# A graph layer with a mixture of experts on one core: rows turned by transposing DMAs instead of TensorE

## Chip, cores and metric

One NeuronCore of a Trainium2 chip runs the whole layer as one program. The metric is the device time of one execution in microseconds (us).

## What is computed

The reference, cut to the parts that the change touches (1250 tokens of 1024 features, 8 experts of which each token takes 2):

```python
xn = _layernorm(x)
x = x + gnn(xn, edges) + mix(xn, W_qkv, ..., W_out, b_out)      # graph product and linear attention
z = _layernorm(x)
t = z * rsqrt(mean(z * z) + 1e-5) * norm_scale                  # rows that gate and experts read
logits = t @ gate_w + gate_b                                    # 1024 x 8
top_v, top_i = top_k(logits, 2); probs = softmax(top_v)
for each expert e:
    h = swiglu(t @ w1[e] + b1[e])                               # 1024 -> 512 -> 256
    y = h @ w2[e] + b2[e]                                       # 256 -> 1024
    acc = acc + w[:, e] * y
out = x + z + acc
```

Float32 in and out. Large products are made of f16 halves: a value is a high part plus a low part, and three products (high-high, high-low, low-high) stand for one.

## The kernel before

Five engines run programs of their own and meet at semaphores; each engine takes its instructions strictly in the order in which they are written, so the order inside the loops below is the schedule. SyncE (SP) issues plain DMAs, GpSimd (POOL) does some sums and issues the gathers and the adding scatters. Two stages matter here.

**The mix stage**, tiles of TT = 125 tokens, i = 2 to 9 in a loop (tiles 0 and 1 are started in the stage ahead). In `mix_tile` TensorE adds 96 products of 512 columns for tile i (`graph_part`, L933, and `attend_part`, L939), with four small float32 products `attend_unit` (L890) for a later tile between them; tiles 8 and 9 have none. Beside it:

- VectorE: four times `attend_unit` (L1686 to L1688: add, reciprocal, multiply), `add_half` twice (L1723, takes TensorE's sums out of a bank; TensorE waits for it before it writes that bank again), `mix_norm(i - 1)` (L1727 to L1741), which makes the rows t of the tile before in `tm` and raises `t_ready`, and `gate` (L1745).
- In the same tile 4 to 6 *quarters* of expert weights are split for later use, 40 in all: SP asks for a float32 quarter (`quarter_ask`, L535, two buffers), ScalarE writes its high half (L1322), VectorE its low half (L1749), and SP stores both (`next_quarters`, L541) and asks for the next but one.
- ScalarE: `attend_hi` (L1272), two small roots, and `tt_copy` (L1316). POOL: `attend_lo` (L639), `mix_out` (L655, on which the store of the base rows waits) and `mix_in` (L651, adds the bias to the x rows of the next tile).
- The gate: `gate_tile` (L987) turns tile i - 1 of t by eight float32 transposes on TensorE into PSUM, ScalarE copies them to `tt`, and `gate_logits` (L994) makes the logits by eight float32 products of 8 columns. SP stores t and the base rows (`store_mixed`, L395), and t is read back by the experts.

Then the routing works out which token goes where.

**The expert stage**: 27 blocks of 128 rows. For block b: POOL gathers 128 rows of t (`gather`, L696) into one of two buffers `rows`; TensorE turns them by eight float32 transposes (`row_T`, L1024) into PSUM; ScalarE copies the f16 high half (`row_hi`, L1359), VectorE the low half (`row_lo`, L1880) to `rowT`; TensorE multiplies, 24 products in two halves (`up`, L1033); VectorE and ScalarE apply swiglu; TensorE turns the result (`act_T`, L1041) between the halves of the next block's `up`, ScalarE and VectorE split it (L1364, L1899), and `down` is 12 products (L1051). VectorE evacuates (L1907), ScalarE scales by the gate's weight (`scale_y`, L1373), and POOL adds the rows to the output by an accumulating scatter (`add_block`, L706). Each scatter waits for the one before to have landed (`y_added`). TensorE's order in a block is `row_T(b + 1)`, first half of `up(b)`, `act_T(b - 1)`, second half of `up(b)`, `down(b - 1)`. POOL's is: wait for the buffer, `gather(b + 2)`, `add_block(b - 2)`. Weights of an expert are loaded by SP while the experts before run.

## Time and profile before

| | us |
|---|---|
| median of 3 runs | 1025.75 |
| the runs | 1019.88 to 1029.12 |
| profiled execution, its own time | 1022.55 |
| its span, first to last instruction | 1020.8 |
| mix stage, tiles 2 to 9 (from t of tile 1 to t of tile 9) | 511 to 716 |
| expert stage (from the first turned row to the end) | 752 to 1021 |

The profile lists for each engine when it was busy and what ended its waits. A busy TensorE is not one at its peak; a wait is put down to whatever signal came last. The chain of waits is followed back from the last instruction, so it names what set the end, while busy shares are means over stages.

### The profile page before, as it was taken

How to read it: one execution, taken by the hardware profiler on the slowest of the kernel's cores; microseconds unless marked ns; L12 is line 12 of the kernel's file. 1: busy time of each engine (PE TensorE's matmuls, PEld its weight loads, DVE VectorE, ACT ScalarE, POOL GpSimd, SP SyncE). 2: the span in 40 equal slices, each digit the busy share in tenths (PEclk: the TensorE clock that was granted, in tenths of full speed). 3: DMA queues.
4: the chain of work that ended last, by engine and by line, in shares of the span. 5: the costliest groups of instructions: out<-in, count | busy, mean ns of one | idle time of the engine just before them, and what ended most of it. 6: DMA issues, size and time to landing. Idle time of an engine off the chain costs nothing.

```text
span 1020.8 us, 16203 instructions
## 1 busy us (share of the span) xinstructions
PE 922.0 (90%) x5361; PEld 576.2 (56%) x5362; DVE 708.9 (69%) x1198; ACT 366.5 (36%) x621; POOL 173.5 (17%) x210
## 2 busy tenths in 40 slices
PE   3998999999999999998998999998359999999992
PEld 2555667766665654555665666665335455555551
DVE  4867999999999974378856777755455455555551
ACT  5657666666441114431122222222112233333331
POOL 1000000000000000015222223322122233323322
PEclk9999999999999999999999999999569999999997
DMA  9735676666663009910255555566459978886544
GB/s 303 227 92 167 201 221 213 194 195 191 213 199 123 22 22 231 336 53 1 61 163 148 159 161 158 151 175 172 177 197 311 315 185 251 270 252 144 123 83 62
DMA packets 89162, 176.59 MB, mean 173 GB/s; under 512 B 24824, under 2 KB 39160, under 8 KB 89088
## 3 DMA queue, kind: packets, MB, share of 16 engines
q1 hardware_dynamic: 81328, 147.50, 46.1%
q0 software_dynamic: 7776, 28.32, 12.4%
q8 instruction: 37, 0.61, 0.3%
q14 instruction: 21, 0.17, 0.1%
HBM read 113.63 MB, written 62.67 MB: 173 GB/s over the span
## 4 chain that ended last, share of the span: by engine, by line
PE 41%; DVE 20%; DMA 18%; ACT 6%; issue 5%; POOL 4%; SPq 3%; DVEq 1%; POOLq 0%; ACTq 0%
PE bank L758 10%; PE windows L1033 9%; DMA arena<-in_w_flat 7%; PE bank L907 7%; DMA arena<-t_dram,arena 6%; PE bank L1051 4%; DVE arena L1687 2%; POOL arena L655 2%; DMA out_x<-arena 2%; DVE arena L1510 2%; PE bank L1024 2%; SPq L541 2%; DMA arena<-in_w_qkv 2%; PE windows L790 2%; DVE arena L1520 2%
## 5 line engine op out<-in xcount | busy, mean ns | idle before, releaser
L758 PE MATMUL bank<-arena 128*125 128x512 f16 x960 | 217.0, 384 | 10.2 <-DVE arena L1483 10.2
L758 PEld LDWEIGHTS bank<-arena 128*125 128x125 f16 x960 | 130.5, 138 | 84.2 <-issue 11.3
L1033 PE MATMUL windows<-arena 128*128 x648 | 149.5, 381 | 0.0
L907 PE MATMUL bank<-arena 128*128 128x416 f16 (+1 forms) x576 | 105.7, 338 | 2.0 <-DMA arena<-split_dram 2.0
L1033 PEld LDWEIGHTS windows<-arena 128*128 128x128 f16 x648 | 63.7, 98 | 65.6 <-issue 1.4
L933 PE MATMUL bank<-arena 128*125 128x512 f16 x432 | 96.3, 379 | 3.8 <-DVE arena L1723 2.3
L939 PE MATMUL bank<-arena 128*125 128x512 f16 x432 | 97.5, 384 | 0.0
L1749 DVE SCALAR_TENSOR_TENSOR arena<-arena 128x512 f16<-128x512 f32 x40 | 39.3, 982 | 61.8 <-ACT arena L1322 61.8
L907 PEld LDWEIGHTS bank<-arena 128*128 128x128 f16 x576 | 55.0, 97 | 45.5 <-DMA arena<-split_dram 2.4
L933 PEld LDWEIGHTS bank<-arena 128*125 128x125 f16 x432 | 58.7, 137 | 37.8 <-DVE arena L1723 2.7
L939 PEld LDWEIGHTS bank<-arena 128*125 128x125 f16 x432 | 59.7, 138 | 34.3 <-issue 1.6
L1051 PE MATMUL bank<-arena 128*128 x324 | 74.3, 379 | 2.2 <-DVE arena L1899 2.2
L639 POOL TENSOR_TENSOR arena<-arena 128x250 f16<-128x250 f32 x40 | 26.6, 665 | 261.1 <-ACT arena L1272 261.1
L1687 DVE RECIPROCAL arena<-arena 128x250 f32<-128x250 f32 x40 | 68.7, 1717 | 1.4
L706 POOL DMA_INDIRECT out_x<-arena x27 | 43.3, 1605 | 150.6 <-ACT arena L1373 88.2
L1272 ACT ACTIVATE arena<-arena 128x250 f16<-128x250 f32 x40 | 16.5, 412 | 140.7 <-DVE arena L1688 140.7
L1510 DVE TENSOR_TENSOR arena<-windows,arena 128x1024 f32 x49 | 59.7, 1219 | 6.8 <-PE windows L791 3.9
L1359 ACT ACTIVATE arena<-bank 128x512 f16<-128x512 f32 x54 | 29.3, 594 | 78.7 <-PE bank L1024 71.0
L790 PE MATMUL windows<-arena 128*128 128x128 f16 x392 | 50.6, 219 | 5.4 <-ACT windows L1188 5.2
L1887 DVE SCALAR_TENSOR_TENSOR arena<-windows,arena 128x512 f32<-128x512 f32 x27 | 18.7, 691 | 51.7 <-PE windows L1033 51.7
L1051 PEld LDWEIGHTS bank<-arena 128*128 128x128 f16 x324 | 31.7, 98 | 40.4 <-issue 2.5
L1520 DVE SCALAR_TENSOR_TENSOR arena<-arena 128x1024 f16<-128x1024 f32 x44 | 53.5, 1216 | 1.1 <-ACT arena L1133 1.1
(248 smaller groups left out, 1428.1 us busy)
## 6 DMA issues: line engine op xcount, KB each, us to landing
arena<-split_dram SPq DMA_DIRECT2D x56, 512.0 KB, 5.5
arena<-in_w_flat SPq DMA_DIRECT2D x44, 512.0 KB, 4.5
split_dram<-arena SPq DMA_DIRECT2D x88, 256.0 KB, 4.6
arena<-in_w_flat SPq DMA_DIRECT2D x40, 256.0 KB, 4.5
split_dram<-arena SPq DMA_DIRECT2D x80, 128.0 KB, 2.3
arena<-in_x SPq DMA_DIRECT2D x20, 448.0 KB
arena<-in_w_qkv SPq DMA_DIRECT2D x8, 1024.0 KB, 11.7
t_dram<-arena SPq DMA_DIRECT2D x10, 448.0 KB
```

Source lines behind the costliest of these rows:

```text
L706: pool.indirect_dma_start(out=out, out_offset=bass.IndirectOffsetOnAxis(ap=to_idx[s], axis=0), in_=ysb[s], in_offset=None, compute_op=ALU. ...
L758: mm = pe.matmul(bank[b][0:TT, :], xt[:, l, k, tok(i)], wkv[:, r, k, c0:c0 + 512], start=(k == 0 and n == 0), stop=(k == KT - 1 and n == 2))
L790: pe.matmul(o, key_hi, lo, start=False, stop=False, skip_group_check=True)
L907: mm = pe.matmul(bank[u % 3][:, 0:n], wq[h][:, l, k, :], xt[:, r, k, a:a + n], start=(k == 0 and c == 0), stop=(k == KT - 1 and c == 2))
L933: pe.matmul(o[half][0:TT, :], xt[:, l, k, tok(i)], wg[:, r, k, c0:c0 + 512], start=(k == 0 and c == 0), stop=False)
L939: mm = pe.matmul(o[half][0:TT, :], ut16[:, k, bass.ds(2 * t + l, 1), h * TT:(h + 1) * TT].rearrange("p o n -> p (o n)"), wo[:, r, k, c0:c0 ...
L1033: mm = pe.matmul(bank[6][:, :], rowT[s][:, l, k, :], arena16[:, bass.ds(off + (r * KT + k) * 512, 512)], start=(k == 0 and c == 0), stop=( ...
L1051: mm = pe.matmul(bank[half][:, :], actT[:, l, k, :], arena16[:, bass.ds(off + 8192 + r * 2048 + k * D + half * 512, 512)], start=(k == 0 a ...
L1510: v.tensor_tensor(w_acc[:, bass.ds(at[0], G * P)], windows[:, :], w_acc[:, bass.ds(at[0], G * P)], ALU.add).then_inc(acc_done, 1)
L1520: v.scalar_tensor_tensor(part[h][:, 1, :], stage[h], SW, part[h][:, 0, :], ALU.mult, ALU.subtract).then_inc(piece_done, 1)
L1687: st.done(v.reciprocal(a, a))
L1749: v.scalar_tensor_tensor(quarter_part[q % 2][:, 1, :], quarter[q % 2], SW, quarter_part[q % 2][:, 0, :], ALU.mult, ALU.subtract).then_inc( ...
```

## The change

Both turns leave TensorE and become DMAs of a crossbar, issued by ScalarE's queue, which write the turned f16 data to SBUF directly.

- Mix stage: t is split into f16 halves before it is turned: `split_hi` on ScalarE (one copy of 1024 columns) and `split_lo` on VectorE (one subtraction of 1024) write `t_hl`, which SP stores in place of the float32 rows (the same bytes). `gate_turn` turns [128, 2048] f16 in one DMA. The logits are sixteen f16 products: eight of 16 columns, the high half with both halves of the gate's weights, and eight of 8 columns. `gate` is two instructions. `gate_tile` and `tt_copy` are gone.
- In SP's `next_quarters` the ask for the next but one quarter stands ahead of the two stores.
- POOL zeroes `t_hl` once, ahead of the sum of the biases, since 3 of its 128 partitions hold no token.
- VectorE's and ScalarE's orders in a mix tile are new (rows below). TensorE does `gate_logits(0)` ahead of tile 2, and `gate_logits(i - 1)` behind tile i.
- Expert stage: `turn` turns the gathered [128, 2048] f16 rows in one DMA to `rowT`. `row_T`, `row_hi` and `row_lo` are gone. POOL waits for the turn in place of TensorE before it gathers into a buffer again, and `up` waits for the turn.

```diff
-            def gate_tile(i, h):
-                pe.wait_ge(t_ready, i + 1)
...
-                    mm = pe.transpose(bank[4 + k // 4][:, (k % 4) * TT:(k % 4 + 1) * TT], tm[h][0:TT, k * P:(k + 1) * P], ident[0:TT, 0:TT])
...
             def gate_logits(i):
-                pe.wait_ge(tt_done, 2 * (i + 1))
+                pe.wait_ge(tt_in, 16 * (i + 1))
                 pe.wait_ge(gate_done, START + i)
                 for k in range(KT):
-                    mm = pe.matmul(bank[6][0:TT, 0:E], tt[:, k, :], gate_f[:, k * E:(k + 1) * E], start=(k == 0), stop=(k == KT - 1))
+                    pe.matmul(bank[6][0:TT, 0:2 * E], tt[:, k, 0:TT], gate16[:, k, :], start=(k == 0), stop=False)
+                for k in range(KT):
+                    mm = pe.matmul(bank[6][0:TT, 0:E], tt[:, KT + k, 0:TT], gate16[:, k, 0:E], start=False, stop=(k == KT - 1))
                 mm.then_inc(gate_mm, 1)
-            gate_tile(0, 0)
-            pe.wait_ge(mixc_in, 80)
+            pe.wait_ge(gate_lo, 1)
+            gate_logits(0)
             for i in range(2, NT):
                 mix_tile(i, i % 2, i // 2, attend=i < NT - 2)
-                gate_logits(i - 2)
-                gate_tile(i - 1, 1 - i % 2)
...
+                gate_logits(i - 1)
             gate_logits(NT - 1)
...
+            def gate_turn(i):
+                a_.wait_ge(t_lo, i + 1)
                 a_.wait_ge(gate_mm, START + i)
...
+                a_.dma_start_transpose(tt, t_hl[i % 2].rearrange("p a b -> p (a b)")).then_inc(tt_in, 16)
...
                 for q in qs:
                     sp.wait_ge(quarter_lo, q + 1)
+                    if q + 2 < QUARTERS:
+                        quarter_ask(q + 2)
                     for hl in range(2):
                         sp.dma_start(quarter_rows(split_dram[hl], q), quarter_part[q % 2][:, hl, :]).then_inc(quarter_out[q % 2], 16)
-                    if q + 2 < QUARTERS:
-                        quarter_ask(q + 2)
...
+            pool.wait_ge(m_mm, 2 * KT)
+            for h in range(2):
+                pool.memset(t_hl[h], 0.0).then_inc(t_clear, 1)
...
-                    pool.wait_ge(rt_psum, 2 * t + h + 1)
+                    pool.wait_ge(turn_in[h], 16 * (t + 1))
                     gather(2 * t + h + 2, h)
                     add_block(2 * t + h - 2, h)
...
-            def row_hi(b, s, first=False):
-                a_.wait_ge(rt_psum, b + 1)
+            def turn(b, s, q, first=False):
+
+                a_.wait_ge(row_in[s], 16 * (q + 1))
                 if not first:
                     a_.wait_ge(h_mm, b - 1)
...
+                a_.dma_start_transpose(rowT[s], rows[s]).then_inc(turn_in[s], 16)
...
-                    row_hi(b + 1, 1 - h)
+                    turn(b + 1, 1 - h, t + 1 + h)
                     act_hi(b - 1)
                     scale_y(b - 2, h)
                     sigmoid(b)
```

VectorE, a mix tile with `attend_unit` (L1686 to L1688), from `gate` (L1745) on; L1749 is a quarter's low half, L1723 `add_half`. Before:

```order
L1745 SCALAR_TENSOR_TENSOR arena<-windows,arena 125x8
L1749 SCALAR_TENSOR_TENSOR arena<-arena 128x512
L1686 TENSOR_TENSOR arena<-bank,arena 128x250
L1687 RECIPROCAL arena<-arena 128x250
L1688 SCALAR_TENSOR_TENSOR arena<-arena 128x250
L1749 SCALAR_TENSOR_TENSOR arena<-arena 128x512
L1686 TENSOR_TENSOR arena<-bank,arena 128x250
L1687 RECIPROCAL arena<-arena 128x250
L1688 SCALAR_TENSOR_TENSOR arena<-arena 128x250
L1749 SCALAR_TENSOR_TENSOR arena<-arena 128x512
L1723 SCALAR_TENSOR_TENSOR arena<-bank,arena 125x512
```

The same stretch of the changed kernel, behind its `gate`; there L1690 to L1692 are `attend_unit`, L1749 is `split_lo`, L1758 a quarter's low half, L1727 `add_half`:

```order
L1690 TENSOR_TENSOR arena<-bank,arena 128x250
L1691 RECIPROCAL arena<-arena 128x250
L1692 SCALAR_TENSOR_TENSOR arena<-arena 128x250
L1749 TENSOR_TENSOR arena<-arena 125x1024
L1690 TENSOR_TENSOR arena<-bank,arena 128x250
L1691 RECIPROCAL arena<-arena 128x250
L1692 SCALAR_TENSOR_TENSOR arena<-arena 128x250
L1758 SCALAR_TENSOR_TENSOR arena<-arena 128x512 x2
L1690 TENSOR_TENSOR arena<-bank,arena 128x250
L1691 RECIPROCAL arena<-arena 128x250
L1692 SCALAR_TENSOR_TENSOR arena<-arena 128x250
L1758 SCALAR_TENSOR_TENSOR arena<-arena 128x512 x2
```

The first quarter now stands behind two attend units and `split_lo`, the quarters come in pairs, four of them stand ahead of the first `add_half` where three did, and the attend unit that stood ahead of `mix_norm` stands behind it.

ScalarE, one block of the expert loop (L1359 `row_hi`, L1364 `act_hi`, L1373 `scale_y`, L1369 the sigmoid). Before:

```order
L1359 ACTIVATE arena<-bank 128x512 x2
L1363 REGISTER_ALU
L1364 ACTIVATE arena<-windows 128x256
L1373 ISA
L1373 ACTIVATE arena<-arena 128x1024
L1367 REGISTER_ALU
L1369 ACTIVATE arena<-arena 128x256
```

And of the changed kernel (L1368 `act_hi`, L1377 `scale_y`, L1373 the sigmoid):

```order
L1363 DMA_TRANSPOSE arena<-arena 128x16x128
L1367 REGISTER_ALU
L1368 ACTIVATE arena<-windows 128x256
L1377 ISA
L1377 ACTIVATE arena<-arena 128x1024
L1371 REGISTER_ALU
L1373 ACTIVATE arena<-arena 128x256
```

The issue of the turn stands where the two copies stood, ahead of `act_hi`.

## Rows read from the trace of the kernel before

**Rows 1.** The page: busy time of each engine.
```profile
PE 922.0 (90%) x5361; PEld 576.2 (56%) x5362; DVE 708.9 (69%) x1198; ACT 366.5 (36%) x621; POOL 173.5 (17%) x210
```
**Rows 2.** By stretch: length, busy PE, PEld, DVE, ACT, POOL (instructions), PE clock, DMA share, GB/s.
```profile
595.70:622.60 26.90, 25.50 (x130) 17.14 (x128) 19.97 (x28) 6.00 (x13) 8.21 (x6) 1.00 0.57 155
848.00:857.00 9.00, 9.00 (x48) 4.76 (x47) 5.57 (x12) 3.14 (x6) 3.11 (x4) 1.00 0.98 311
962.00:971.00 9.00, 9.00 (x48) 4.76 (x47) 5.18 (x11) 2.92 (x5) 3.34 (x5) 1.00 0.53 117
```
**Rows 3.** Timeline, a mix tile: start, length, engine, line, count [idle before, releaser].
```profile
595.71 1.29 DVE L1741 SCALAR_TENSOR_TENSOR arena<-arena 125x1024 f32<-125x1024 f32 x1
...
597.08 2.81 POOL L655 TENSOR_TENSOR arena<-arena 125x1024 f32<-125x1024 f32 x1 [3.43 <-DVE arena L1741]
...
599.91 0.77 SPq L395 DMA_DIRECT2D out_x<-arena  x2
...
601.20 0.73 DVE L1749 SCALAR_TENSOR_TENSOR arena<-arena 128x512 f16<-128x512 f32 x1 [1.00 <-ACT arena L1322]
...
602.21 0.43 SPq L535 DMA_DIRECT2D arena<-in_w_flat  x1
...
603.10 0.78 SPq L395 DMA_DIRECT2D arena<-in_x  x2
...
607.84 0.63 ACT L1322 ACTIVATE arena<-arena 128x512 f16<-128x512 f32 x1 [2.93 <-DMA arena<-in_w_flat]
608.50 0.69 DVE L1749 SCALAR_TENSOR_TENSOR arena<-arena 128x512 f16<-128x512 f32 x1 [4.04 <-ACT arena L1322]
...
609.85 0.69 PE L890 MATMUL bank<-arena 128*128 128x250 f32 x2 [1.17 <-DVE arena L1723]
...
614.58 2.24 DVE L1749 SCALAR_TENSOR_TENSOR arena<-arena 128x512 f16<-128x512 f32 x1
...
622.60 1.29 DVE L1741 SCALAR_TENSOR_TENSOR arena<-arena 125x1024 f32<-125x1024 f32 x1
```
**Rows 4.** The chain of waits: start, length, what.
```profile
144.72 1.37 PE bank L765 x24
...
469.19 2.32 POOL arena L646
...
714.73 1.28 DVE arena L1741
...
722.66 3.54 PE windows L994 x16
...
873.96 9.55 DMA arena<-t_dram,arena
...
892.63 0.87 PE bank L1024 x8
893.51 2.59 PE windows L1033 x12
...
995.95 6.08 DMA out_x<-arena
```
**Rows 5.** Timeline of POOL in the expert stage: two scatters.
```profile
882.02 1.60 POOL L706 DMA_INDIRECT out_x<-arena  x1 [6.86 <-DMA out_x<-arena]
...
889.99 1.61 POOL L706 DMA_INDIRECT out_x<-arena  x1 [4.15 <-ACT arena L1373]
```
**Rows 6.** Groups by line: count | busy, mean ns of one | idle before.
```profile
L1669 DVE TENSOR_TENSOR arena<-arena 128x1024 f16<-128x1024 f32 x8 | 9.4, 1221 | 1.3 <-ACT arena L1262 1.3
...
L628 POOL MEMSET arena<- 128x1024 f32 x1 | 1.0, 952 | 295.3 <-PE bank L758 295.3
```
**Rows 7.** DMA issues over the span: count, KB each, median us to landing.
```profile
arena<-split_dram SPq DMA_DIRECT2D x56, 512.0 KB, 5.5
...
wg_dram<-arena SPq DMA_DIRECT2D x16, 256.0 KB, 3.8
...
arena<-in_kn_w SPq DMA_DIRECT2D x1, 512.0 KB, 14.0
```

More of the change, by code:

```diff
@@ L1341, in _ @@
+                quarter_split(qs[0])
+                gate_turn(i - 1)
+                quarter_split(qs[1])
+                if attend:
+                    attend_hi(4 * h + 2, t + 1, unit + 2)
+                for q in qs[2:4]:
                     quarter_split(q)
[L1342 to L1345 removed]
+                if attend:
+                    attend_hi(4 * h + 3, t + 1, unit + 3)
```

165 lines of the change are left out of this document (73 added, 92 removed).

## The prediction

> **What bounds the kernel now.** I read the page first. TensorE is busy for 90% of the span [rows 1], which invites the reading that whatever leaves TensorE leaves the time. The stretches and the chain say where that holds.
>
> In the mix stage it does not quite. A tile takes 26.9 us and TensorE is busy for 25.50 of them [rows 2] (from one finished t to the next, 595.71 to 622.60 [rows 3]), but it waits 1.17 us in each tile for VectorE's `add_half` [rows 3]. `add_half` was late because it is queued behind a quarter: VectorE idled 4.04 us for ScalarE, which had idled for the quarter's DMA, asked for at 602.21 and landed 5.6 us later, at 607.8 [rows 3]. So one tile of VectorE is 19.97 us of work [rows 2], 6.0 of waits for quarters (4.04, and twice the 1.00 that a quarter waits right behind an attend unit, because ScalarE must first do `attend_hi` and then the quarter's high half [rows 3]) and 0.9 of small gaps: 26.9. VectorE with the quarters' round trip is the loop that closes last; TensorE has hardly more than a microsecond in hand.
>
> In the expert stage TensorE does set the pace. The chain runs over `row_T` (0.87), and three groups of twelve products at 2.59 [rows 4], with 0.2 for `act_T` a block of 8.86 us. But a second loop is close: each scatter waits for the one before. Alone it lands in 6.08 us [rows 4], and with 0.9 for POOL's wake-up, index and issue that is 7.0 from one to the next. At 882.02 a scatter had waited 6.86 us for the one before it; the next, 7.97 us later, waited for ScalarE, so the one in flight had then landed in under 7.2 [rows 5]. And a gather of 9.55 us ended on the chain [rows 4], so gathers are no earlier than needed. DMA is 0.98 busy where weights load and 0.53 in late blocks [rows 2].
>
> **The change, part by part.**
>
> *TensorE in a mix tile.* Eight float32 logits go, 1.77 us at full clock (half of the 3.54 that they took at half clock [rows 4]), and eight turns, 0.87 like those of a block [rows 4]. Sixteen f16 products come; 24 narrow f16 ones took 1.37 us, 57 ns each [rows 4], so 0.9. TensorE's work falls from 25.5 to 23.8 us. That is worth nothing in time while VectorE's tile is longer.
>
> *VectorE in a mix tile.* It gains `split_lo`, 1.22 us by its like [rows 6], and 0.2 for the second gate instruction: 21.4. The row of 2.24 us [rows 3] is a quarter stretched by POOL's sum beside it, which now falls behind the quarters: 1.55 less, so 19.8, with the gaps 20.7. The waits in the new order, counted from a finished t: gate 0.3, attend unit 2.5 (between the end of the first quarter, about 597.7, and 600.2, where the wait of 1.00 begins [rows 3]), `split_lo` 1.2, attend unit 2.5, wait 1.0 for ScalarE, quarter 0.7: the first quarter ends at 8.2. The second waits 0.45 (the turn's issue stands between, taken like SP's 0.43 [rows 3]) and ends at 9.3, the attend unit behind it at 11.9. The third quarter was asked for at 8.3, now ahead of its stores. I take 4.2 us to land, between 3.8 [rows 7] and the 5.6 above; with ScalarE's 0.63 it is there at 13.1: wait 1.2. The fourth is held up in SP's queue. Ahead of its ask stand the x rows, which wait until the base rows have landed, and these wait for POOL's sum of 2.81 [rows 3], now queued behind an `attend_lo` whose attend unit comes after t: the sum ends at 6.9, the store lands 3.2 after its issue (599.91 to 603.10 [rows 3]) at 10.1, the x rows' issue takes 0.8, and 5.6 later, at 16.5, the fourth quarter lands. With 0.7 for ScalarE it is ready at 17.2, VectorE at 14.0: wait 3.2. The fifth stands right behind an attend unit: 1.0. Waits 6.9, tile 20.7 + 6.9 = 27.6: 0.7 more than 26.9, in six tiles +4. Lower bound: the fourth quarter lands with the third, tile 24.4, six tiles -15; TensorE's 23.8 would stop it there. Upper: the last quarter still meets POOL's sum, +1.55 a tile, +13. In tiles 8 and 9, without attend units, the earlier ask and `split_lo` about cancel.
>
> *Ahead of tile 2.* `gate_logits(0)` now waits for a first turn. TensorE can spare this, but VectorE stands at `gate(0)` and the next attend unit: two halves of t at 1.22 each, 0.45, 5.5 to land and 0.9 of products are 9.3 us from its last work on tile 1, of which it fills 7 with `mix_norm`, `split_lo` and the gate's weights: +2. With a turn that lands in 14.0 [rows 7] it would be +10.
> POOL's zeroing is two fills of 4 KB a partition, 0.95 each [rows 6], ahead of a sum that is on the chain [rows 4]: +2, +4 if f16 costs by the element, 0 if an attend unit hides it.
>
> *Behind tile 9.* Before, from t (714.73 + 1.28) to the end of the last logits (722.66 + 3.54) 10.2 us [rows 4]. Now 1.2 + 1.2 + 0.45 + 5.5, and 1.8 of products at half clock, 10.2: nothing. With 3.8 to land -1.7, with 14.0 +8.5.
>
> *Expert stage.* TensorE's block is 8.86 - 0.87 = 8.0. ScalarE's and VectorE's two copies go, which nothing waited for. A turn needs three prices, none of which the trace shows. To land: 5.5, like the other 512 KB [rows 7], between 3.8 and 14.0. Of the DMA engines: at 311 GB/s with a share of 0.98 [rows 2] 512 KB are 1.7 us. Of ScalarE's queue: 0.45, at most twice the 1.6 of a scatter's issue [rows 5], 3.2. Late blocks have room: 0.53 x 9 = 4.8 us of DMA work and 1.7 are 6.5 in 8.0, and the scatter, 7.0 from one to the next, becomes at most 8.7. The turn is used a block after its gather lands, so 9.55 + 0.5 + 5.5 = 15.5 us fit into the two blocks (16.0) that a gather has; the buffer is free again just as late. In about 17 blocks I give TensorE its 0.87: -15. In the other ten or so weights load, the DMA engines are full [rows 2], and 512 KB more must be paid: some +1 each, since the loads themselves have slack, +10. The first block waits for a gather and a turn in place of a gather and copies: +2. Sum -3. Both ends: 27 x 0.87 = -23; and all 27 blocks at a scatter of 8.7 + 1.7 are +40.
>
> *A rule of the skill here.* The Trainium skill, "DMA: Bandwidth & Descriptors", section "Latency and other measured facts", gives 261 GB/s for a transposing DMA with a non-contiguous middle dimension. By that 512 KB are an estimated 2.0 us of the engines against my 1.7, so +3 in the ten loaded blocks. No run here shows it yet.
>
> **Sum.** Against the profiled execution, 1022.55 us: +4 +2 +2 +0 -3 = +5, 1027.6. That execution lies 3.2 below the median of the runs (1025.75); I put the new time at 1028, which is no change as far as a measurement of this kernel can tell (about 1%).
>
> **Rivals.**
>
> *A, faster.* The quarters land early enough and TensorE becomes the bound in both stages. For it: the ask stands ahead of the stores, an earlier `add_half` is what the 1.17 us of TensorE ask for [rows 3], and late blocks have DMA to spare [rows 2]. Against it: SP's queue behind the x rows, as worked out, and a scatter loop that is already at 7 to 8 us. Time: six tiles at 24.4 or so, -15 (in place of +4), the expert stage -15, the fixed +4 and 0 of the tail: -26, near 997; with half of either gain near 1010.
>
> *B, slower by the issue.* ScalarE is held for 3.2 us by each turn's issue. In a mix tile that stands between two quarters (+1.5 a tile after what the fourth quarter's wait absorbs, +12); in a block it stands ahead of `act_hi`, which is due 2.8 us after the block starts (one 2.59 and `act_T`). The gather lands about when the block starts, so the issue ends 0.4 late, up to 1 where gathers are late: 27 x 0.8 = +21. Time 1028 + 33 = 1061. It decides from an issue of about 2.5 us on. For it: a turn has more pieces than any plain DMA here. Against: a plain issue of 128 rows takes 0.43.
>
> *C, slower by the crossbar.* A turn takes 14 us or more. Then gather, turn and release of a buffer are a loop, (9.55 + 0.5 + 14 + 1.5) / 2 = 12.8 us a block, 27 x 3.9 = +105, with +8 and +8 at the two ends of the mix stage: near 1145. It decides from about 6 us on, above which each microsecond costs half of one a block. For and against it no row speaks but the 14.0.
> The Trainium skill, "VectorE: DVE Perf Modes", section "The three transpose paths", has 1309 ns for one 128x128 f16-sized block through the crossbar and 390 ns on TensorE. If sixteen went one behind another, the estimate would be 20.9 us a turn, which is this case and worse; if that figure is mostly fixed cost, it is my case. No run here tells yet.
>
> **How the numbers follow.** Chances: my forecast 0.35 (its own range 1014 to 1042), A 0.33, B 0.21, C 0.11. Of the forecast's share 0.22 lies within 1%, 0.10 above and 0.03 below; of A 0.02 within. Faster 0.34, within 1% 0.24, slower 0.42. The range leaves out C and the best end of A: 1000 to 1075.
>
> **What would show it.** In the mix stage: intervals between finished t of 27 to 28 us against 26.9, TensorE's work near 24 in each with some 4 idle before L890 or the graph products, and VectorE's longest wait ahead of the fourth quarter. If the interval is 25 or less, my reading of SP's queue is wrong. In the expert stage: blocks of 8.0 us late and 9 to 11 where weights load; scatters that wait for the one before more often than seven times in 27; the issue row of the turn under 0.6 us on ScalarE, its landing near 5.5. An issue above 2.5 is B, blocks of 11 us or more also late, with TensorE waiting for the turn, is C. POOL's two fills and the first turn should show as 4 us ahead of t of tile 1 and tile 2.

## The result: 11% slower, and the profile after

| | before | after |
|---|---|---|
| median, us | 1027.37 | 1147.6 |
| the runs | 1019.88 to 1029.12 | 1134.43 to 1173.72 |
| ratio | | 1.114 [1.105, 1.122] |
| profiled execution, its own time | 1022.55 | 1173.72 |

I had forecast 1028 with a range of 1000 to 1075. That is wrong: the time lies 120 us above the forecast and 73 above the range. The profiled execution after is the longest of its four, by 25 us and more; the other three alone enter the ratio. Its rows show mechanisms; how much each part costs is taken from the timed runs below.

The page after: busy time, the span in 40 slices (TensorE's clock and the DMA engines), and the queue that carries the turns. The same row of before is in [rows 1].

```profile
PE 929.4 (79%) x5065; PEld 550.9 (47%) x5066; DVE 689.8 (59%) x1165; ACT 338.6 (29%) x558; POOL 174.9 (15%) x212
...
PEclk9999999999999999879899998855888966888997
DMA  9454677666510891026666666646999999998984
...
DMA packets 166122, 195.98 MB, mean 167 GB/s; under 512 B 101785, under 2 KB 116121, under 8 KB 166049
...
q10 hardware_dynamic: 76960, 19.40, 13.4%
```

TensorE is as busy as before, 929 us against 922, although it does 296 instructions fewer: its granted clock falls in both stages. The 37 turns are 76,960 packets, 2080 each. Their packets took 13.4% of 1172 us, which is 157 us of all sixteen engines or 4.2 us a turn, where I had 1.7. (This "engine time" is the time that packets took by the profile. It is no fixed price, as the runs below show.) In the expert stage the DMA row stands at 9 nearly throughout.

The groups of the page that lost most, busy and mean ns of one, then the idle time before them and what ended it:

```profile
L1023 PE MATMUL windows<-arena 128*128 x648 | 165.1, 410 | 85.9 <-DMA arena<-arena 84.3
...
L1041 PE MATMUL bank<-arena 128*128 x324 | 85.2, 419 | 22.2 <-DVE arena L1898 22.2
...
L1758 DVE SCALAR_TENSOR_TENSOR arena<-arena 128x512 f16<-128x512 f32 x40 | 32.1, 802 | 77.4 <-ACT arena L1315 77.4
```

L1023 is `up`. TensorE waits 84 us for turns (`arena<-arena`) and 22 us for the split of act, which waits for ScalarE. In the mix stage VectorE waits for quarters.

One mix tile after, to be laid beside [rows 3] (timeline: start, length, engine, line, count [idle before, releaser]); t of two tiles stands first and last, L1303 is the turn's issue, L1315 and L1758 the halves of a quarter, L1727 `add_half`:

```profile
557.12 1.28 DVE L1745 SCALAR_TENSOR_TENSOR arena<-arena 125x1024 f32<-125x1024 f32 x1
...
565.67 4.20 ACTq L1303 DMA_TRANSPOSE arena<-arena  x1
...
569.97 0.63 ACT L1315 ACTIVATE arena<-arena 128x512 f16<-128x512 f32 x1 [3.55 <-issue]
...
570.63 0.69 DVE L1758 SCALAR_TENSOR_TENSOR arena<-arena 128x512 f16<-128x512 f32 x1 [3.45 <-ACT arena L1315]
...
578.73 0.63 ACT L1315 ACTIVATE arena<-arena 128x512 f16<-128x512 f32 x1 [3.92 <-DMA split_dram<-arena]
...
579.39 0.69 DVE L1758 SCALAR_TENSOR_TENSOR arena<-arena 128x512 f16<-128x512 f32 x1 [3.81 <-ACT arena L1315]
580.00 0.68 DVE L1727 SCALAR_TENSOR_TENSOR arena<-bank,arena 125x512 f32<-125x512 f32 x1
...
580.74 1.20 PE L896 MATMUL bank<-arena 128*128 128x250 f32 x2 [5.34 <-DVE arena L1727]
...
581.74 7.72 PE L939 MATMUL bank<-arena 128*125 128x512 f16 x24
...
588.92 1.28 DVE L1745 SCALAR_TENSOR_TENSOR arena<-arena 125x1024 f32<-125x1024 f32 x1
```

The tile takes 31.8 us (26.9 before). The issue takes 4.20 us of ScalarE, so VectorE waits 3.45 us for the second quarter. It waits 3.81 us for the fourth, because ScalarE waits for the *store* of the quarter two before it. `add_half` stands behind both, and TensorE waits 5.34 us. Its granted clock is then low, 0.64 from 580.7 to 588.7 us: 24 products take 7.72 us, where 24 like them take 5.34 us at a clock of 1.00.

### The profile page after: what moved, and what is told of

Its sections match the earlier page's. It is cut to its first block, busy times and chain, and to the rows that moved or that the text cites. A ratio compares the mean times of both kernels' runs of the same rounds, so it can differ in the third digit from the quotient of the medians.

```text
span 1172.0 us, 15535 instructions
## 1 busy us (share of the span) xinstructions
PE 929.4 (79%) x5065; PEld 550.9 (47%) x5066; DVE 689.8 (59%) x1165; ACT 338.6 (29%) x558; POOL 174.9 (15%) x212
## 3 DMA queue, kind: packets, MB, share of 16 engines
q10 hardware_dynamic: 76960, 19.40, 13.4%
q0 software_dynamic: 7776, 28.32, 12.1%
## 4 chain that ended last, share of the span: by engine, by line
PE 31%; DMA 28%; DVE 20%; issue 7%; ACT 6%; ACTq 3%; POOL 2%; SPq 2%; DVEq 1%; POOLq 0%
DMA arena<-arena 12%; PE bank L764 9%; DMA arena<-t_dram,arena 7%; PE bank L913 6%; DMA split_dram<-arena 5%; PE windows L1023 4%; DVE arena L1691 3%; ACTq L1363 3%; PE bank L939 3%; PE bank L945 2%; DMA arena<-in_w_qkv 2%; DVE arena L1514 2%; DVE arena L1524 1%; DMA out_x<-arena 1%; PE bank L1041 1%
## 5 line engine op out<-in xcount | busy, mean ns | idle before, releaser
L1023 PE MATMUL windows<-arena 128*128 x648 | 165.1, 410 | 85.9 <-DMA arena<-arena 84.3
L764 PE MATMUL bank<-arena 128*125 128x512 f16 x960 | 217.4, 384 | 11.1 <-DVE arena L1487 11.1
L764 PEld LDWEIGHTS bank<-arena 128*125 128x125 f16 x960 | 130.6, 138 | 85.4 <-issue 12.3
L1023 PEld LDWEIGHTS windows<-arena 128*128 128x128 f16 x648 | 67.5, 104 | 171.4 <-issue 113.9
L939 PE MATMUL bank<-arena 128*125 128x512 f16 x432 | 113.1, 426 | 12.8 <-DVE arena L1727 11.3
L1898 DVE TENSOR_TENSOR arena<-windows,arena 128x256 f16<-128x256 f32 x27 | 11.4, 424 | 167.1 <-ACT arena L1368 167.1
L1041 PE MATMUL bank<-arena 128*128 x324 | 85.2, 419 | 22.2 <-DVE arena L1898 22.2
L945 PE MATMUL bank<-arena 128*125 128x512 f16 x432 | 98.4, 386 | 0.0
L939 PEld LDWEIGHTS bank<-arena 128*125 128x125 f16 x432 | 66.8, 155 | 56.5 <-issue 18.6
L913 PEld LDWEIGHTS bank<-arena 128*128 128x128 f16 x576 | 55.8, 98 | 47.3 <-issue 3.0
L1758 DVE SCALAR_TENSOR_TENSOR arena<-arena 128x512 f16<-128x512 f32 x40 | 32.1, 802 | 77.4 <-ACT arena L1315 77.4
L1368 ACT ACTIVATE arena<-windows 128x256 f16<-128x256 f32 x27 | 10.3, 383 | 232.5 <-PE windows L1031 133.8
L945 PEld LDWEIGHTS bank<-arena 128*125 128x125 f16 x432 | 60.2, 139 | 35.0 <-issue 2.5
L642 POOL TENSOR_TENSOR arena<-arena 128x250 f16<-128x250 f32 x40 | 29.2, 730 | 307.1 <-ACT arena L1259 307.1
L1041 PEld LDWEIGHTS bank<-arena 128*128 128x128 f16 x324 | 34.0, 105 | 68.8 <-issue 38.3
## 6 DMA issues: line engine op xcount, KB each, us to landing
arena<-in_w_qkv SPq DMA_DIRECT2D x8, 1024.0 KB, 11.3
```

Of the source, the lines that this page charges most:

```text
L764: mm = pe.matmul(bank[b][0:TT, :], xt[:, l, k, tok(i)], wkv[:, r, k, c0:c0 + 512], start=(k == 0 and n == 0), stop=(k == KT - 1 and n == 2))
L913: mm = pe.matmul(bank[u % 3][:, 0:n], wq[h][:, l, k, :], xt[:, r, k, a:a + n], start=(k == 0 and c == 0), stop=(k == KT - 1 and c == 2))
L939: pe.matmul(o[half][0:TT, :], xt[:, l, k, tok(i)], wg[:, r, k, c0:c0 + 512], start=(k == 0 and c == 0), stop=False)
L945: mm = pe.matmul(o[half][0:TT, :], ut16[:, k, bass.ds(2 * t + l, 1), h * TT:(h + 1) * TT].rearrange("p o n -> p (o n)"), wo[:, r, k, c0:c0 ...
L1023: mm = pe.matmul(bank[6][:, :], rowT[s][:, l * KT + k, :], arena16[:, bass.ds(off + (r * KT + k) * 512, 512)], start=(k == 0 and c == 0), ...
L1041: mm = pe.matmul(bank[half][:, :], actT[:, l, k, :], arena16[:, bass.ds(off + 8192 + r * 2048 + k * D + half * 512, 512)], start=(k == 0 a ...
```

## Experiments: where the 120 us are

First the split between the stages, then the mix stage, then the experts. Edits are against the changed kernel unless said otherwise; lines left out of a cut are marked "...". A ratio is to the kernel before, run beside the experiment; its median was 1024 to 1026 us each time. The theories: S, the issue of a turn holds ScalarE; O, the new order of VectorE makes TensorE wait; D, a turn takes too much of the DMA engines, which are full; Q, of these, above all in the queue of an expert's weights; L, gather and turn one behind the other are too long for two buffers.

**Old experts (`e1_old_experts`).** The new mix stage, the experts of before.

```diff
+                for k in range(KT):
+                    mm = pe.transpose(bank[2 + 2 * s + k // 4][:, (k % 4) * P:(k % 4 + 1) * P], rows[s][:, k * P:(k + 1) * P], ident)
...
-                a_.dma_start_transpose(rowT[s], rows[s]).then_inc(turn_in[s], 16)
```

> The new mix stage with the experts of before (eight float32 turns on TensorE, float32 rows of t stored), so that the loss is split between the two stages. In the profile of the changed kernel t of tile 9 comes 47.8 us later than before, and the last logits another 5 us: all theories put this run near 1025 + 53 = 1078 us (1065 to 1085), and the experts' share then is the other 65 us. If it is under 1050 most of the loss in the mix stage belongs to something else than the change (a disturbed profile), if over 1100 the experts lost little.

Measured 1070.1, ratio 1.046 [1.040, 1.052]. The mix stage costs 44 us, the experts the other 76 (I had read 65 from the profiles).

**Turned by TensorE in the mix stage too (`e3_tensor_turn`).** e1 with the float32 turn and logits of before.

```diff
+                    mm = pe.transpose(bank[4 + k // 4][:, (k % 4) * TT:(k % 4 + 1) * TT], tm[h][0:TT, k * P:(k + 1) * P], ident[0:TT, 0:TT])
...
-                a_.dma_start_transpose(tt, t_hl[i % 2].rearrange("p a b -> p (a b)")).then_inc(tt_in, 16)
```

> As e1, but t is turned on TensorE and the logits are the float32 products of before; the new order on VectorE and ScalarE, the ask ahead of the stores, both halves of t (still computed, read by nobody) and the zeroing stay. Theory S (the turn's issue, about 4 us, holds ScalarE between two quarters and in front of the first root): the turn is gone, so only the zeroing (3.6 us) and the halves of t (up to 1.2 us a tile) are left: 1030 to 1040. Theory O (the new order of VectorE puts its waits in front of TensorE, whoever turns): the tiles stay at 30 us and more, 1060 or above.

1049.3, 1.024 [1.019, 1.029]: between the two. The turn, with the f16 logits that hang on it, is 21 us of the 44, and 23 remain without any turning DMA, more than S and less than O had said.

**Before, with the ask ahead of the stores (`e5_before_ask_ahead`).**

```diff
                     sp.wait_ge(quarter_lo, q + 1)
+                    if q + 2 < QUARTERS:
+                        quarter_ask(q + 2)
                     for hl in range(2):
                         sp.dma_start(quarter_rows(split_dram[hl], q), quarter_part[q % 2][:, hl, :]).then_inc(quarter_out[q % 2], 16)
-                    if q + 2 < QUARTERS:
-                        quarter_ask(q + 2)
```

> The kernel before with one edit: SP asks for the next but one quarter ahead of the two stores. In e3 ScalarE waited 27 us in five tiles for the stores of a quarter to land (before: for the quarter's own DMA, 38 us). If the ask ahead of the stores is part of the 24 us that e3 loses: slower than before by 5 to 15 us, 1031 to 1041. If the new order of VectorE is all of it: 1022 to 1030.

A miss in sign: 1012.6, ratio 0.988 [0.983, 0.992]. This one edit of the change is a gain of 13 us and beats both kernels. Between 540 and 700 us TensorE is now busy for 159.6 of the 160 us (150.6 before), so it is the bound there.

**The new order alone (`e14_order_alone`).** e5 and the new order of VectorE and ScalarE.

```diff
-                quarter_split(qs[2])
...
+                for q in qs[2:4]:
+                    quarter_split(q)
                 add_half(i, h, 0)
-                attend_unit(4 * h + 3, t + 1, unit + 3)
-                quarter_split(qs[3])
-                add_half(i, h, 1)
+                if attend:
+                    attend_unit(4 * h + 3, t + 1, unit + 3)
```

> The kernel before with the ask ahead of the stores (e5, 1012.6 us) and the new order of VectorE and ScalarE in a mix tile, without the halves of t and without the zeroing: all that stands between e5 and e3 (1049.3) but these two. Theory O (the pair of quarters ahead of the first add_half makes TensorE wait): most of the 36.7 us are here, 1035 to 1045. If the halves of t (VectorE 1.2 us, ScalarE 1.0 a tile) and the zeroing (3.6 us) are most of it: under 1028.

1039.4, 1.015 [1.011, 1.018]: the order costs 27 us, the halves of t and the zeroing the other 10. Waits from 540 to 700 us in e5, then in e14 (who waited, for whom, us in total, times, longest; L1749 and L1769 are a quarter's low half, L1322 and L1332 its high half, L1739 is `add_half`):

```profile
ACT arena L1322 <- DMA split_dram<-arena: 39.0, 16, 8.4
DVE arena L1749 <- ACT arena L1322: 38.1, 22, 6.3
...
PE bank L890 <- DVE arena L1688: 0.2, 1, 0.2
```
```profile
DVE arena L1769 <- ACT arena L1332: 45.3, 21, 7.0
ACT arena L1332 <- DMA split_dram<-arena: 33.5, 11, 10.4
...
PE bank L894 <- DVE arena L1739: 8.2, 4, 2.2
```

In e5 TensorE waits for next to nothing. In e14 it waits 8.2 us for `add_half`, which stands behind two quarters in a row, and 2.1 us for attend units, and its granted clock is 0.95 in this stretch against 1.00. ScalarE waits for stores in both, no longer in e14 (33.5 us) than in e5 (39.0), so it is not these waits by themselves that cost, but where they stand. There are two quarter buffers, and each is free only when its store has landed. With an attend unit between two quarters (the old order) VectorE has work in that time; with two pairs ahead of `add_half` the wait falls in front of it. That the pairing does it is argued from these rows; I did not move it by itself.

**SP issues the turn in the mix stage (`e2_sp_turn`).** e1 with the issue moved off ScalarE.

```diff
             def store_mixed(i):
                 h = i % 2
+                sp.wait_ge(t_lo, i + 1)
+                sp.wait_ge(gate_mm, START + i)
+                apart(sp)
+                sp.dma_start_transpose(tt, t_hl[h].rearrange("p a b -> p (a b)")).then_inc(tt_in, 16)
```

> e1 with the turn of the mix stage issued by SP (ahead of the store of t) in place of ScalarE, and earlier by up to 5 us. Theory S: ScalarE no longer stands 4 us between two quarters; SP's queue stands instead, ahead of the stores and asks, where some of it comes back: faster than e1 by 5 to 15 us, 1055 to 1065. Theory D (the turn's packets delay the quarter's own transfers): within 4 us of e1, 1066 to 1074. If SP's queue is the scarcer one (my reading of the fourth quarter): slower, over 1075.

1063.9, 6 us less than e1. The place on ScalarE is at most a third or so of the turn's 21, since more has moved than the place: SP issues the turn earlier, and it then takes 1.6 us to issue and 3.7 to land at the median, against 4.0 and 8.2 in the changed kernel. What the 15 us are that stay with so short a turn, the runs do not show.

**The f16 logits without the turning DMA (`e18_narrow_logits`).** e5, TensorE turns, ScalarE and VectorE split the turned rows.

```diff
+                    ins = v.tensor_tensor(tt[:, 1, 4 * b:4 * b + 4, :], bank[4 + b][:, 0:4 * TT].rearrange("p (k n) -> p k n", n=TT),
+                                          tt[:, 0, 4 * b:4 * b + 4, :], ALU.subtract)
```

> A version meant to be faster than both kernels: e5 (before with the ask ahead, 1012.6 us; TensorE there hardly waits any more in a mix tile) with the sixteen f16 products of the change but the turns on TensorE: ScalarE copies the high half of the turned rows out of PSUM, VectorE subtracts the low half (some 1.3 us a tile, where it has 38 us of waits in six tiles). TensorE's tile is 0.9 us shorter: eight tiles, less 1.5 behind the last one: 1005 to 1010. If VectorE with the quarters closes last again: 1012 to 1020.

1019.3, 0.994 [0.992, 0.996]: better than before, not than e5. The tiles with attend units take 26.2 us (25.3 to 26.2 in e5). TensorE waits 9.3 us for VectorE's attend units between 540 and 700 us, where e5 had 0.2: the 0.9 us a tile that TensorE saves are worth nothing while VectorE gains work.

**The ladder (`e13_ladder`).** The price of a turn alone, in the routing stage of before.

```diff
+            for cols in (2048, 0, 1024, 512, 128, 2048):
+                if cols:
+                    a_.dma_start_transpose(bias_b.bitcast(F16)[:, 0:cols].rearrange("p (k n) -> p k n", n=P), scale_b.bitcast(F16)[:, 0:cols]).then_inc(spare_turn, 16)
+                else:
+                    a_.dma_start(bias_b, scale_b).then_inc(spare_turn, 16)
```

> The kernel before, with six transfers one behind another (each waited for) on ScalarE's queue during the routing, when the other queues are nearly quiet: turns of 2048 columns, a plain copy of 512 KB, turns of 1024, 512, 128 and again 2048 columns. If the 4 us of the issue and 8 us to land in the mix stage are the price of a turn's own packets: issue 4, 2, 1, 0.4 us and landing 8, 5, 3.5, 2.5, in proportion to the columns plus some 2 us. If they come from other transfers beside it: here the issue of 2048 columns is under 2 us and lands in 4 (the shortest of the mix stage landed in 3.9 with an issue of 1.6). The time of the kernel stays at 1026 or rises by up to 10, where the ladder reaches into the first gathers.

The issues on ScalarE's queue (start, length), then for the stretches of the first three the packets, MB and share of the sixteen engines, and the time to land:

```profile
729.86 1.44 ACTq L1359 DMA_TRANSPOSE arena<-arena  x1
734.25 0.53 ACTq L1361 DMA_DIRECT2D arena<-arena  x1
737.23 1.26 ACTq L1359 DMA_TRANSPOSE arena<-arena  x1
```
```profile
q10 hardware_dynamic: 2080, 0.52, 62.8%
...
arena<-arena ACTq DMA_TRANSPOSE x1, 4.4
...
q10 hardware_dynamic: 144, 0.52, 42.6%
...
arena<-arena ACTq DMA_DIRECT2D x1, 512.0 KB, 3.0
...
q10 hardware_dynamic: 1056, 0.26, 43.9%
...
arena<-arena ACTq DMA_TRANSPOSE x1, 3.1
```

Alone, a turn holds ScalarE for 1.44 us, lands in 4.4 and takes 0.628 x 4.4 = 2.8 us of the engines (the second of 2048 columns, last in the ladder: 2.02 us and 4.3); the plain copy takes 0.426 x 3.0 = 1.3. The kernel's time stayed at 1026.5. The second guess was right: the 4 us and 8 us of the mix stage come from what is under way beside it. A turn alone is cheap against those, though more than twice the plain copy, and its 2.8 us of the engines are already above my 1.7.

**Smaller weight loads (`e7_after_small_loads`).** It leaves out nearly all weights of experts 3 to 7 and computes with what the buffers hold.

```diff
-                        sp.dma_start(to, split_dram[hl, m + n]).then_inc(s, 16)
+                        if e < 3:
+                            sp.dma_start(to, split_dram[hl, m + n]).then_inc(s, 16)
+                        else:
+                            sp.dma_start(to[:, 0:16], split_dram[hl, m + n, :, 0:16]).then_inc(s, 16)
```

> The changed kernel with nearly all of the weights of experts 3 to 7 left out (16 of 2048 columns are loaded, the buffers keep older weights), so the engines carry no loads in most of the expert stage. Leaves out work. Theory Q: blocks of 8.0 to 8.5 us from expert 2 on, no wait of TensorE for a turn over 3 us, issues of 1.5 to 3 us: 1075 to 1095 in all. Theory S: an issue of 4 us in front of the copy of act to f16 stays in each block, so blocks stay at 9.5 or more: 1115 or above.

1127.1 in a single run: only some 20 us less, and TensorE still waited 61.7 us for turns, in 17 waits of up to 12.1. Q's burst of weight packets is not the main cause. The stretch from 880 to 1080 us, with hardly a weight under way, and its queues of gathers and scatters (q0) and of turns (q10), columns as in [rows 2] and as in the page above:

```profile
880.00:1080.00 200.00, 167.56 (x728) 74.87 (x726) 71.24 (x152) 34.88 (x57) 58.02 (x77) 0.93 1.00 166
...
q0 software_dynamic: 5510, 20.08, 52.4%
q10 hardware_dynamic: 38820, 9.78, 41.0%
```

The DMA share is 1.00 all the same. These are 19 blocks and 38,820 / 2080 = 18.7 turns, so gather and scatter take 0.524 x 200 / 19 = 5.5 us of the engines a block and a turn 0.41 x 200 / 18.7 = 4.4, together 9.9 us, where TensorE needs 8.0. This fits theory D without Q.

**Paced loads (`e6_paced_loads`).**

```diff
                         sp.dma_start(to, split_dram[hl, m + n]).then_inc(s, 16)
+                        if e > 0:
+                            sp.wait_ge(s, 128 * e + 16 * (3 * hl + n + 1))
```

> The changed kernel, in which the loads of an expert's weights (from expert 1 on) wait for each other: one piece of 512 KB is under way at a time instead of six and two biases. Theory Q (the turn's 2080 packets of 256 bytes stand in the DMA engines' queues behind the packets of the loads, so it lands after 14 to 24 us while six pieces are under way): the waits of 15 to 18 us of TensorE go, some 40 us less, near 1100, and the longest wait of TensorE for a turn is under 8 us. Theory S (what costs is the 4 us on ScalarE's queue): no change, 1135 to 1150. If the pieces one by one no longer keep up with the experts, TensorE waits for a weight instead, and the time rises.

1213.5, 1.189 [1.181, 1.197], slower still. The waits for turns fell from 84 to 54 us, the longest to 11.3 (Q had under 8), but TensorE then waited 78 us for weights: pieces one at a time do not keep up.

**A turn nobody needs (`e9_extra_turn`), and the same issued later (`e15_extra_behind`).** e1 and one more turn, of zeros, in 24 blocks; e15 has it behind `scale_y`.

```diff
                     row_hi(b + 1, 1 - h)
+                    a_.wait_ge(spare_turn, 16 * (b - 1))
+                    extra_turn()
                     act_hi(b - 1)
                     scale_y(b - 2, h)
```

> e1 (experts as before, TensorE turns) with one more turning DMA of [128, 2048] f16 in each of 24 blocks, of zeros, into memory that nobody reads: only ScalarE waits, for the one a block earlier. Theory D (the sixteen DMA engines are full: by the profile a turn takes 4.6 us of all of them, gather and scatter 5, loads 3 a block, together more than a block of 8.9): near e1 + 24 x (11.5 - 8.9) = 1070 + 62 = 1132 us (1115 to 1145), although nothing needs the turn. Theory L (gather, turn and release of the buffer are a loop, and its length is what costs): e1 + 0 to 10, at most 1080. Theory S (ScalarE is held by the issue ahead of its copy of act): e1 + 24 x 1 = about 1095.

> e9 (1197 us) with the extra turn issued behind ScalarE's copy of act and its scaling of y, not ahead of them. In e9 TensorE waited 49 us for the split of act (ScalarE was in the issue for up to 12 us) and 57 us for gathers that landed late. Theory S (the time on ScalarE's queue): the 49 us and what hangs on them go, 1130 to 1150. Theory D (the turn's packets slow every other transfer; ScalarE's waits only follow): 1180 or more.

e9 1196.9, 1.160 [1.148, 1.171]; e15 1124.0, 1.095 [1.084, 1.105]. The extra turn costs 127 us ahead of `act_hi`, more than any theory had, and 54 behind, less than S or D had said for that: a price on ScalarE and one beside it are both there. The flaw of both: ScalarE also waits for the extra turn of one block earlier, 43 us in e9 and 27 in e15.

**Plain copies in its place (`e12_extra_plain`, `e16_extra_pieces`).** Both against e9.

```diff
-                a_.dma_start_transpose(bias_b.bitcast(F16).rearrange("p (k n) -> p k n", n=P), scale_b.bitcast(F16)).then_inc(spare_turn, 16)
+                a_.dma_start(bias_b, scale_b).then_inc(spare_turn, 16)
```
```diff
-                a_.dma_start_transpose(bias_b.bitcast(F16).rearrange("p (k n) -> p k n", n=P), scale_b.bitcast(F16)).then_inc(spare_turn, 16)
+                a_.dma_start(view(198656, [2 * KT, P], F16), view(203552, [2 * KT, 2 * P], F16)[:, :, 0:P]).then_inc(spare_turn, 16)
```

> e9 with the extra turn replaced by a plain copy of the same 512 KB from the same memory to the same memory, issued at the same place by ScalarE's queue. What is in dispute: whether a turn is dear for its bytes or for its 2080 packets of 256 bytes. By bytes (my own price, 1.7 us of the sixteen engines): it would cost about as much as the turn, e9's 1197 less little, 1180 or more. By packets: the copy has few large ones, costs 1.7 us of the engines a block where they are full, so e1 + 10 to 25: 1080 to 1095.

> e12 (plain copy, 1079 us) with the same 512 KB copied in pieces of 256 bytes, 2048 of them, from pieces that lie 512 bytes apart, still without turning. If the price of a turn is that of small packets: near e9, 1170 or more. If it is that of the turning itself (2 bytes at a time through the crossbar, or what the queue does for it): near e12, 1075 to 1100.

The plain copy 1079.2 (+9), the one in pieces 1115.9 (+46), with 59 us of ScalarE's waits for it, the same flaw.

**The flaw mended (`e19_free_turn`, `e20_free_pieces`).** Three places to write to, and a wait for the transfer of three blocks earlier; the cut is e19 against e9. e20 has the plain copy in pieces in the turn's place.

```diff
-                    a_.wait_ge(spare_turn, 16 * (b - 1))
-                    extra_turn()
+                    a_.wait_ge(spare_turn[u % 3], 32 * t + 16 * (u // 3 + 1))
+                    extra_turn(u % 3)
```

> e9 (1197 us) with its flaw mended: there ScalarE waited, ahead of its copy of act, for the extra turn of one block earlier, which late landings made 43 us. Now there are three places to write to, and it waits for the turn of three blocks earlier. What is left is the turn's issue on ScalarE and its share of the DMA engines. If both stay as dear as in e9: 1197 - 43 = 1154 or more. If most of e9 was that wait and what followed from it: 1100 to 1130, near e15 (1124).

> e16 (1116 us, plain pieces of 256 bytes) mended in the same way; its wait for the extra copy was 59 us on ScalarE. If small packets as such slow the other transfers: 1090 or more. If they cost nothing but their own late landing: near e12 (1079), 1072 to 1085; the difference to e19 is then the turning itself, its issue and its engine time.

The turn 1185.7, 1.156 [1.149, 1.164], +116 to e1; the pieces 1080.9, 1.058 [1.052, 1.064], +11. So neither bytes nor small packets are dear here: the same 512 KB in 256-byte pieces cost about what a plain copy costs, 0.5 us a block, the turning 4.8. Stretches of the expert stage of e1, of e20 and of e19 (columns as in [rows 2]; the last three are TensorE's clock, DMA share, GB/s):

```profile
830.00:1030.00 200.00, 195.87 (x1013) 102.42 (x1012) 110.60 (x220) 64.13 (x111) 68.80 (x89) 1.00 0.78 214
```
```profile
830.00:1040.00 210.00, 199.12 (x1014) 103.33 (x1012) 110.25 (x221) 64.27 (x110) 68.58 (x88) 0.98 1.00 264
```
```profile
830.00:1130.00 300.00, 209.48 (x949) 105.02 (x948) 104.47 (x207) 59.88 (x103) 64.22 (x84) 0.84 0.96 173
```

With the pieces the engines are full and move 264 GB/s; with the turns they are as full and move 173. Length times share is the engine time of a stretch: 156 us in e1, 210 in e20, 288 in e19. What e20 adds just fits beside TensorE's work, what e19 adds does not. The queue of the turns and extra transfers on the pages of e1 (which has the ten turns of the mix stage only), e20 and e19:

```profile
q10 hardware_dynamic: 20800, 5.24, 3.4%
```
```profile
q10 hardware_dynamic: 70336, 17.83, 9.0%
```
```profile
q10 hardware_dynamic: 70720, 17.83, 12.4%
```

Less e1's 36 us, a copy in pieces took (97 - 36) / 24 = 2.5 us of the engines and a turn (148 - 36) / 24 = 4.6 (in e15, by the same sum, 3.2). The other transfers slow down too, but less: the packets of the two large queues, the same in all three, took 602 us of the engines in e1, 592 in e20 and 639 in e19. So of what e19 adds to the engines some 111 us are the turns' own and 37 fall on what is beside them. The issues of e20, then of e19, and whom e19 keeps waiting:

```profile
L1379 ACTq DMA_DIRECT2D arena<-arena x24: 601/602/9342, 822.8 to 1041.6; - x24
```
```profile
L1379 ACTq DMA_TRANSPOSE arena<-arena x24: 1334/3988/17157, 821.5 to 1151.4; - x24
...
DMA to landing us min/median/max: 4.3/5.8/35.1
```
```profile
ACT arena L1384 <- issue: 98.2, 14, 16.3
...
PE bank L1051 <- DVE arena L1930: 50.2, 11, 13.0
PE bank L1024 <- DMA arena<-t_dram,arena: 44.9, 5, 14.8
```

A plain copy's issue takes 0.60 us at the median and 9.3 at most, a turn's 3.99 and up to 17.2 (min, median, max in ns). Ahead of its copy of act ScalarE stood 98 us in issues (18 in e20). TensorE waited 50 us for the split of act that follows, and 45 us for gathers that landed late beside the turns. A turn has two prices, and both are paid; how the 116 us divide between them these runs do not tell.

**The issue behind ScalarE's other work (`e10_turn_behind`), in the changed kernel.**

```diff
-                    turn(b + 1, 1 - h, t + 1 + h)
                     act_hi(b - 1)
                     scale_y(b - 2, h)
+                    turn(b + 1, 1 - h, t + 1 + h)
```

> The changed kernel with ScalarE's order in a block altered: the copy of act and the scaling of y first, then the turn. The issue no longer stands ahead of what TensorE's down products and the scatter wait for, but each turn starts up to 4 us later. Theory S: 20 us or more faster, 1120 or less. Theory D: within 10 us of the changed kernel, 1137 to 1157. Theory L: slower by up to 2 us a block where the gather had landed early, 1150 to 1190.

1155.2, 1.125 [1.118, 1.132]: against S, and what D and L both allowed. The wait for the split of act falls from 22.2 to 2.2 us, and nothing is gained: TensorE needs the turn itself, later now, and waits 96 us for it.

**A third row buffer (`e17_third_buffer`).**

```diff
-        rows = [T2([2 * D], F16) for _ in range(2)]
...
+        rows = [T2([2 * D], F16) for _ in range(3)]
```

> The changed kernel with a third buffer for gathered rows, so that each gather is asked for a block earlier. Theory L (gather and turn one behind the other take longer than the two blocks that two buffers give): most of TensorE's 84 us of waits for turns go, 1090 to 1110. Theory D (the DMA engines are full while weights load, and what is asked for earlier lands no earlier): within 15 us of the changed kernel, 1130 to 1155.

1125.3, 1.098 [1.089, 1.107]: about 21 us less, more than D and less than L had said, with the waits for turns down from 84 to some 50. The chain of gather and turn over two buffers is a part; 55 of the experts' 76 us stay.

**Half a turn (`e11_half_turn`).** It leaves out the low half of the rows.

```diff
-                a_.dma_start_transpose(rowT[s], rows[s]).then_inc(turn_in[s], 16)
+                a_.dma_start_transpose(rowT[s][:, 0:KT], rows[s][:, 0:D]).then_inc(turn_in[s], 16)
```

> The changed kernel with only the high half of the rows turned in the experts (1024 of 2048 columns, half of the packets); the products take the high half in place of the low one, the same number of products. Leaves out work. Theory D: 2.3 us less of the engines a block, 27 x 2.3 = 62 less, near 1085 (1075 to 1100), DMA still over 0.9 busy. Theory L: the landing halves, the block comes near 8.5: 1070 to 1080. Theory S: the issue falls from 4 to 2 us: 1120 or so.

1106.3, 1.078 [1.072, 1.085]: 40 us less, between D and S. The issue's median falls from 3.6 to 1.37 us, and of the 76 us about half go with half of the data.

## Why the prediction was wrong, step by step

The sum that the runs give: 1026 - 13 (ask) + 27 (order) + 10 (halves of t, zeroing) + 21 (turns in the mix stage) + 76 (experts) = 1147. Each term is the step from one kernel to the next, so the sum must close; it shows where the time lies and proves nothing more, and a term is good to a few us. My own sum had +4 for the mix tiles, +2 and +2 ahead of tile 2, and -3 for the experts. It also started from the profiled execution, 1022.55, and never added the 3.2 by which this lay below the median, a slip that is small beside the rest.

**The expert stage: the step that failed is the price of the turn.** I had put 1.7 us of the engines, 5.5 to land and 0.45 of ScalarE, worked out from other 512 KB transfers. The changed kernel shows 157 / 37 = 4.2 us of the engines over all turns. With that my own sum would have spoken: 0.53 x 9 = 4.8 us of a late block and 4.2 are 9.0, more than the 8.0 that I gave the block (e7 measures 9.9 without weights), and where weights load there was no room at all. "Late blocks have room", the step that gave -15, was false. The stretch from 850 to 1150 us, and four long steps in a row of the chain there (start, length):

```profile
850.00:1150.00 300.00, 215.07 (x907) 95.17 (x906) 88.85 (x190) 44.05 (x72) 69.86 (x92) 0.86 0.98 185
```
```profile
921.76 23.49 DMA arena<-arena
946.39 15.73 DMA arena<-t_dram,arena
962.29 32.62 DMA arena<-arena
996.05 13.68 DMA arena<-t_dram,arena
```

Gather, turn, gather, turn: the loop of rival C, at a DMA share of 0.98. Here a turn took 23 and 33 us (I had 14.0 as an upper end), a gather 14 to 16. These are the worst: the median landing of the experts' turns was 5.0 us in e10, 8.0 in e17 and 9.1 in e7, whose traces give it. Before this, from 837 to 909 us, the chain runs over four issues of 6.3, 8.6, 9.9 and 4.8 us instead, which is rival B's mechanism. What was right: TensorE's block. Between the waits it is 8.0 us; this stretch is one, fully busy:

```profile
1079.80:1087.80 8.00, 8.00 (x40) 3.74 (x39) 3.76 (x8) 1.84 (x3) 3.00 (x4) 1.00 0.82 168
```

So the 0.87 us that leave TensorE are gained, 27 x 0.87 = 23 us, and then the waits (84 + 22 us in the profiled execution) and the low clock that follows them are paid. Rival C's 1145 is near the result by luck: it has 105 us in the experts and 16 at the ends of the mix stage, and the runs give 76 and 44.

**The issue.** I took 0.45 us, at most 3.2 (rival B). The mix stage has a median of 4.0, the experts 3.6 and up to 14.1. B's mechanism is there, with its price above my upper end, though taking the issue out of the way in the experts alone gained nothing (e10); I had named its point of decision, 2.5 us, and given it 0.21 for want of a row. In the mix stage it is the second quarter's wait: 3.45 us against my 0.45.

**The order in a mix tile.** My tile was 27.6; without turns (e3) it is 28.1 to 29.4, with them 30.2 to 31.8. VectorE's work in the tile above came out 0.8 us higher than said (20.59 against 19.8), the waits 3.4 higher: 1.00, 3.45, 0.99, 3.81, 1.00 against 1.0, 0.45, 1.2, 3.2, 1.0. The fourth has nearly my size by luck, from another cause: not the ask behind the x rows, but the store of the quarter two before, which ScalarE must see landed; I had not counted that wait at all. And I compared with 26.9 only. What I should have asked is what each of two edits does by itself: the ask alone takes the tile to 25.3 to 26.2 (e5), rival A's way, and the new order takes that away again and more.

**TensorE's clock.** I had left it out of the mix stage. After the wait of 5.34 us the next 24 products took 7.72 us; in this tile 2.4 us come on top of the wait. From 540 to 700 us the granted clock is 0.90 after, and 1.00 before.

**The ends.** Ahead of tile 2 I had +2 for the first turn; from t of tile 1 to t of tile 2 it is 39.6 us against 31.9, +8, since it landed in 7.2 and not 5.5, VectorE waited 1.28 us (0.36 before) for a root behind its issue, and TensorE, idle for 10 us, came back at a granted clock of 0.50. Zeroing: two fills of 1.8 us, 3.6 in all against 2 (my upper bound had 4), and t of tile 0 comes 3.9 us later in e3 than in e14. Behind tile 9 I had nothing: from t to the last logits it is 14.3 us against 10.2, +4, with a turn of 8.8 us beside expert 0's weights.

**The two figures cited.** The 261 GB/s of the Trainium skill, "DMA: Bandwidth & Descriptors", section "Latency and other measured facts", would be an estimated 2.0 us a turn. Alone, a turn shows 0.52 MB in 2.8 us of the engines, 190 GB/s, so that price is 0.8 us too low, and beside other transfers (4.2 us) it is half of the measured one. The 1309 ns of the Trainium skill, "VectorE: DVE Perf Modes", section "The three transpose paths", for one 128x128 block does not add up block by block here: in the ladder 128 columns landed in 2.3 us and sixteen times as many in 4.4. It pointed to rival C, whose loop the trace shows, for a reason that the trace does not bear out.

## What to carry to other kernels

A transfer that is cheap alone is priced by the queue that it joins: before work is moved from an engine to the DMAs, add its engine time to the DMA time of every stage that it joins, and bound it from above by a measured time under load, not by its bytes. Below the length of the stage the addition cost little (e20, +11 us), above it a great deal (e19, +116). A turning DMA held the queue that issued it for 1.4 to 2.0 us alone and for up to 17.2 us beside other transfers, so it is ill placed ahead of anything on a compute engine that others wait for; moving it behind helps only if nobody waits for the turn itself (e15 against e10). And a change of several edits should be priced edit by edit: here one line was worth 13 us (1012.6 against 1026) and the rest lost 134.

## What was not expected of the hardware

A turn fills the DMA engines with little data: with the same 512 KB a block in the same 256-byte pieces they moved 264 GB/s with plain copies and 173 with turns, at a share of 1.00 and 0.96. Most of this is the turn's own engine time, 4.6 us against 2.5 for the pieces; the other transfers took 639 us of the engines against 602. Beside other transfers a turn's engine time was larger, 4.6 us against 2.8 alone, and so was its issue: 1.4 to 2.0 us alone, 4.0 at the median under load, 17.2 at most, where the plain copy in pieces has a median of 0.60 and 9.3 at most. Why is not settled: the runs tell the turning from bytes and from packet size, not what in it does this.
